# Two compares of a sine range reduction and three operations of a rounding chain, given from VectorE to GpSimd, in a two-layer transformer block on eight cores

## What is computed

```python
# layer 0, feed-forward (d_model 1024, d_ff 4096)
hidden = x @ W1 + b1
imag = w_imag * sin(theta + hidden * 0.1)
phase = cos(theta) * w_real + sin(theta) * w_imag
y = relu(hidden + phase * imag * 0.1) @ W2 + b2
# layer 1, attention: K and V are fake-quantized
k = fake_quant(k, scale, zero); v = fake_quant(v, scale, zero)
#   fake_quant: q = clip(round(x / scale + zero), 0, 255); (q - zero) * scale
# layer 1, feed-forward: 16 experts, top 2, plus a shared expert
```

## Time and profile before

| | us |
|---|---|
| median of 2 timed runs | 7583.97 (7529.44 to 7638.49) |
| the profiled execution, its own time | 7332.9 |
| its span, slowest core | 7331.3 |
| its span, fastest core | 7310.8 |
| PE busy, DVE busy, ACT busy, POOL busy | 4706.4, 2767.5, 2083.8, 170.7 |

### The profile page before, as it was taken

The page is one execution under the profiler, slowest core; times in us unless marked ns, Lnnn a source line. Parts: engine busy times, 40 slices in busy tenths (PEclk is TensorE's granted clock), DMA queues, the critical chain, the costliest instruction groups (busy, mean ns, idle before and its releaser), DMA issues.

```text
span 7331.3 us, 65020 instructions; the slowest of 8 cores (7310.8 to 7331.3 us)
## 1 busy us (share of the span) xinstructions
PE 4706.4 (64%) x17489; PEld 1733.7 (24%) x17489; DVE 2767.5 (38%) x4355; ACT 2083.8 (28%) x3175; POOL 170.7 (2%) x186
## 2 busy tenths in 40 slices
PE   1555777873255855735434667773599999998772
PEld 0211222221011311301111122221244444443230
DVE  2524422215544344346434333235433334332114
ACT  2233344533343144222122455633111111111012
POOL 0000000000000000000000000000000000000000
PEclk8777888986565866865556788886799999999885
DMA  1111000000011511400001110000222222222321
GB/s 50 24 18 12 5 8 9 1 12 0 12 19 22 55 20 18 41 12 12 0 0 15 12 12 9 1 12 0 35 35 35 35 35 35 35 35 37 55 46 46
DMA packets 236271, 160.88 MB, mean 22 GB/s; under 512 B 138921, under 2 KB 225494, under 8 KB 233878
## 3 DMA queue, kind: packets, MB, share of 16 engines
q0 software_dynamic: 232320, 138.92, 14.0%
q1 hardware_dynamic: 3606, 17.79, 0.7%
HBM read 287.21 MB, written 8.39 MB: 40 GB/s over the span
## 4 chain that ended last, share of the span: by engine, by line
PE 52%; DVE 25%; ACT 11%; issue 6%; DMA 5%; DVEq 1%; SPq 0%; ACTq 0%; POOL 0%; POOLq 0%
PE ps L305 36%; PE ps L301 15%; DVE SMALLF L323 6%; ACT SQR L332 3%; DVE B1f L323 2%; DVE FQR L323 2%; DVE B4f L323 2%; DMA WBq<-w_qkv 1%; DVE SCpa L323 1%; DVE B2f L323 1%; ACT HID L332 1%; ACT B1f L332 1%; DVE X L323 1%; DMA WBm<-ws_u 1%; ACT SINB L332 1%
## 5 line engine op out<-in xcount | busy, mean ns | idle before, releaser
L305 PE MATMUL ps<-XB,WBm 128*128 128x512 bf16 x4480 | 1117.9, 391 | 64.1 <-DMA WBm<-ws_g 52.8
L305 PE MATMUL ps<-PT,ARV 128*64 128x512 bf16 (+2 forms) x1152 | 485.5, 421 | 391.5 <-DVE XB L323 268.6
L305 PE MATMUL ps<-XB,WBf 128*128 128x512 bf16 x896 | 374.3, 588 | 430.4 <-ACT B0f L332 373.6
L332 ACT ACTIVATE SGR<-ps 128x512 bf16<-128x512 f32 x320 | 191.1, 597 | 1580.8 <-PE ps L301 888.9
L305 PEld LDWEIGHTS ps<-XB,WBm 128*128 128x128 bf16 x4480 | 446.1, 100 | 632.7 <-issue 135.5
L305 PE MATMUL ps<-HPAIR,WBm 128*128 128x512 bf16 x2272 | 546.7, 384 | 59.7 <-DMA WBm<-ws_d 59.7
L332 ACT ACTIVATE PT<-ps,BIASC 128x512 bf16<-128x512 f32 (+3 forms) x640 | 398.9, 623 | 492.8 <-PE ps L301 358.8
L323 DVE TENSOR_TENSOR ps<-ps,CTRI 128x128 f32<-128x128 f32 x512 | 153.5, 300 | 1015.6 <-PE ps L301 987.3
L332 ACT ACTIVATE PT<-ps,BIA 128x512 bf16<-128x512 f32 (+3 forms) x640 | 399.0, 623 | 394.7 <-PE ps L301 227.5
L301 PE MATMUL ps<-PT,CONES 128*128 128x512 bf16 (+3 forms) x1280 | 495.5, 387 | 0.0
L323 DVE RECIPROCAL SMALLF<-ps 64x512 f32<-64x512 f32 x128 | 429.4, 3355 | 65.4 <-PE ps L301 49.6
(11 more groups left out here) (225 smaller groups left out, 5166.7 us busy)
## 6 DMA issues: line engine op xcount, KB each, us to landing
WBf<-w_ff POOLq DMA_DIRECT2D x32, 1024.0 KB, 9.8
WBq<-w_qkv POOLq DMA_DIRECT2D x64, 256.0 KB, 4.7
WBm<-we_g POOLq DMA_DIRECT2D x16, 1024.0 KB, 9.4
WBm<-we_u POOLq DMA_DIRECT2D x16, 1024.0 KB, 13.5
WBm<-we_d POOLq DMA_DIRECT2D x16, 1024.0 KB, 10.7
X<-x SPq DMA_DIRECT2D x1, 8192.0 KB, 34.2
WBkv<-w_qkv POOLq DMA_DIRECT2D x8, 1024.0 KB, 9.3
WBm<-ws_g POOLq DMA_DIRECT2D x8, 1024.0 KB, 8.3
```

The costliest lines, as they stand in the source:

```text
L305: E.matmul(o, l, r, start=a, stop=b, tile_position=t))
L332: getattr(E, nm)(*a, **k).then_inc(sA.h, 1))
```

## The change

A new helper `gop` does for GpSimd what `vop` does for VectorE. In `fakequant` the two casts and the difference go from VectorE to GpSimd, and VectorE's next operation waits for them. In `ffn0` the two compares (`B4` = ...) go to GpSimd, each between operations that stay on VectorE. Added waits keep the buffers safe.

```diff
+        def gop(name, *args, waits=(), **kw):
+            P.em("gpsimd", lambda E, v=sG.n: E.wait_ge(sG.h, v))
+            for (sem, val) in waits:
+                P.wait("gpsimd", sem, val)
+            v = sG.inc()
+            P.em("gpsimd", lambda E, nm=name, a=args, k=kw:
+                 getattr(E, nm)(*a, **k).then_inc(sG.h, 1))
+            return v
...
-                        vop("tensor_copy", FQI[:, :], FQY[:, :], waits=((sA, a1),))
-                        vop("tensor_copy", FQR[:, :], FQI[:, :])
-                        vop("tensor_tensor", FQY[:, :], FQY[:, :], FQR[:, :],
-                            ALU.subtract)
+                        g1 = gop("tensor_copy", FQI[:, :], FQY[:, :],
+                                 waits=((sA, a1), (sV, use.get("fq", 0)),
+                                        (sA, use.get("fq_aev", 0))))
+                        gop("tensor_copy", FQR[:, :], FQI[:, :])
+                        g3 = gop("tensor_tensor", FQY[:, :], FQY[:, :], FQR[:, :],
+                                 ALU.subtract)
                         vop("tensor_scalar", FQC[:, :], FQY[:, :], 0.5, None,
-                            ALU.is_ge)
+                            ALU.is_ge, waits=((sG, g3),))
...
-                                vop("tensor_scalar", B4[:, qsl], B1[:, qsl],
-                                    math.pi, None, ALU.is_ge, waits=((sA, a_t),))
-                                vop("scalar_tensor_tensor", B1[:, qsl], B4[:, qsl],
-                                    -TWO_PI, B1[:, qsl], ALU.mult, ALU.add)
-                                vop("tensor_scalar", B4[:, qsl], B1[:, qsl],
-                                    -math.pi, None, ALU.is_lt)
+                                g1 = gop("tensor_scalar", B4[:, qsl],
+                                         B1[:, qsl], math.pi, None, ALU.is_ge,
+                                         waits=((sA, a_t),))
+                                v1 = vop("scalar_tensor_tensor", B1[:, qsl],
+                                         B4[:, qsl], -TWO_PI, B1[:, qsl],
+                                         ALU.mult, ALU.add, waits=((sG, g1),))
+                                g2 = gop("tensor_scalar", B4[:, qsl], B1[:, qsl],
+                                         -math.pi, None, ALU.is_lt,
+                                         waits=((sV, v1),))
                                 vv = vop("scalar_tensor_tensor", B1[:, qsl],
                                          B4[:, qsl], TWO_PI, B1[:, qsl], ALU.mult,
-                                         ALU.add)
+                                         ALU.add, waits=((sG, g2),))
```

More of the change, by code:

```diff
@@ L694, in fakequant @@
                         use["fq"] = vq
-                        return aop("activation", dst_ap, FQR[:, :], AF.Identity,
-                                   scale=KVC[:, 2:3], bias=KVC[:, 3:4],
-                                   waits=((sV, vq),))
+                        a_ev2 = aop("activation", dst_ap, FQR[:, :], AF.Identity,
+                                    scale=KVC[:, 2:3], bias=KVC[:, 3:4],
+                                    waits=((sV, vq),))
+                        use["fq_aev"] = a_ev2
+                        return a_ev2
                     wq = dram[wqname].rearrange("(c p) n -> p c n", p=128)
```

## The result

The changed kernel is slower: the ratio of its time to that of the kernel before is 1.071, with a 95% interval of 1.060 to 1.082. The median over all timed runs is 8119.3 us (7887.8 to 8310.7, 11 runs); for the kernel before, over 10 runs, 7492.0 us. The forecast was 8072. The spans are 7331.3 us (before) and 7886.7 us (after). The difference to explain is 555 us; the sum on record was 488.

A forecast was written before the change was run, and what follows sets the result against it. Bound: a chain of non-overlapping steps hopping between engines, none full. Compares +197, fakequant +73 and late loads +218 make +488 us on the timed median 7584: 8072 us, range 7700 to 8350.

The forecast's parts named there:

- the sum on record: Whole kernel: compares +197, fakequant +73 and late loads +218 make +488 us.
- The base of 7584: Median of the timed runs before, 251 us above the profiled 7333; the change touches nothing in that distance.
- The chain: ffn0 and fakequant: steps hop between engines without overlap, so added time counts in full, 128 and 64 times.
- Part 1: ffn0's 256 compares on POOL: 0.55 us start, 0.75 work, 0.10 out, 0.77 more each, +197 us.
- My wrong-if bound: ffn0: a POOL compare under 0.45 or over 1.3 us breaks part 1.
- Part 2: fakequant's three moved operations: 3.10 us instead of 1.96 in each of 64 steps, +73 us.
- Part 3: Weight loads queued behind POOL's new work leave late: ffn0 slabs 151, W2 42, K and V 25, +218 us.
- the 26.6 us: Start of W2: third matmul group starts 26.6 us after the last compare instead of 5.4, costing 21.2, twice.
- POOL is as quick as DVE: Rival for the moved operations: they cost nothing extra, late loads remain, +218, 7802 us; 0.16 together with loads not late.
- POOL is dear: Rival for the moved operations: about twice VectorE's ordinary rate, 1.36 us each, +761, 8345 us; chance 0.16.
- The relief counts: Rival: POOL's compare runs beside DVE's other step, DVE loses 248 us of work, 7336 us; chance 0.04.
- The signs I named: ffn0: first-half window 426 to about 600 us, sine wait 4.3, PE idle on WBf about 16 times, some 10 us each.

The follow-up runs named there:

- ffn_only: Against the changed kernel, fakequant's three operations back on VectorE, only ffn0's compares on GpSimd; span 7794.0 us, +463 on the kernel before.
- fq_only: Against the changed kernel, ffn0's compares back on VectorE, only fakequant's three operations on GpSimd; span 7427.6 us, +96 on the kernel before.
- late_loads: Kernel before, all vector work on VectorE, each slab load also waiting for the previous slab's last compare or difference; span 7530.2 us, +199.
- early_loads: Changed kernel with slab loads emitted one slab earlier, ahead of the running slab's GpSimd work; span 7703.7 us, 183 less than the changed kernel.
- pipe_pool: early_loads with ScalarE's and VectorE's lists in ffn0 reordered so steps overlap, compares and fakequant operations still on GpSimd; span 7186.3 us on core 4.
- pipe_casts: Kernel before with overlapping steps in ffn0 and fakequant, only fakequant's two casts on GpSimd, WBkv loads one slab early; ratio 0.917, span 6755.7 us.
- micro: All four stages left out; single operations timed on GpSimd and VectorE, alone and together; GpSimd compare 1.49 us, cast 0.61, VectorE compare 0.43.

## Why the prediction was right, point by point

**The number.** 8072 against 8119 is closer than the reasoning deserves. The sum was 488 us and the spans show 555. The base of 7584 was the median of two runs; over ten it is 7492, and 7492 + 488 would have been 7980. I had said that nothing in the change touches the distance of the timed runs from the profiled one. It was 159 us before (7492 against 7333) and 231 after (8119 against 7888), for which no run here shows a reason. These misses happened to make up for each other.

**The chain.** Right. Every nanosecond between `B0` and the sine went to the end 128 times, in `fakequant` 64 times. `ffn_only` and `fq_only` show the parts to be additive.

**Part 1, the compares: the mechanism right, the term mis-sized by 89 us, from two errors of opposite sign.** I took 0.55 us to get in and 0.75 of work. Measured: 0.15 and 1.49, so 0.40 too much and 0.74 too little, 256 times. The 0.55 came from a load's issue; it is real for a load (0.54 in `late_loads`) and wrong for an ordinary operation. The 0.75 came from the middle of ordinary rows on other engines, and one of them misled: the 0.90 us of `X<-X,COLS` is a mean of two kinds. Timelines of DVE and POOL of the kernel before:

```profile
2451.97 1.65 DVE L323 TENSOR_SCALAR X<-X,COLS 128x512 f32<-128x512 f32 x1 [0.18 <-DVE X L323]
...
2458.88 0.49 DVE L323 TENSOR_SCALAR X<-X,COLS 128x512 f32<-128x512 f32 x1 [0.18 <-DVE X L323]
```

```profile
2451.71 1.68 POOL L277 DMA_DIRECT2D WBf<-w_ff  x1 [12.29 <-PE ps L301]
```

It takes 0.49 us alone and 1.65 while GpSimd issues a load, which itself takes 1.68 us where others take 0.87. The row was no price of an operation but one of a collision, and it stood in the trace before. My wrong-if bound (a compare over 1.3 us breaks part 1) was crossed: part 1 as priced is broken, its place in the chain is not.

**Part 2, fakequant.** +70 for +73, by luck in its inside: 0.19 to get in instead of 0.55, casts 0.61, difference 1.26, together 3.06 us from `FQY`'s end to VectorE's next operation for my 3.10.

**Part 3, the late loads.** Right in all three places, 196 for 218. `late_loads` shows 199 us of it without any GpSimd work, `early_loads` gives 183 back. The surplus was the 0.55 us delay, which a load behind GpSimd's own work does not pay, and a landing of 8.9 to 9.4 us in the slabs where I used the median 9.8. At W2 the 26.6 us came out to the digit, but by luck: the load landed 11.2 us after its start, not 9.8, and the cold group took 8.36, not 9.35.

**The rivals.** "POOL is as quick as DVE" fell. "POOL is dear" held for the work of a compare, 1.49 us where it said 1.36, and not for the casts (0.61); with the short start a compare cost 1.75 us in the chain, between my 1.40 and its 2.01. On the Trainium skill (GPSIMD Engine Reference, § 3.1 Elementwise): its ratio of 1.96 is for a two-input operation, and for that one this trace agrees, 1.26 us against 0.69, a ratio of 1.8; for an operation with a constant the ratio here is 1.49 to 0.43, or 3.5, and for a cast 1.4. "The relief counts" fell in the order of the program, and for the compares in the order of `pipe_pool` too; it holds for the casts in `pipe_casts`.

**The signs I named.** The window over the first half grew to about 635 us, where I wrote 600; ACT's sine waits 4.98 for my 4.3; PE waited for `WBf` 17 times, 16 of them with the load right behind a compare. But I had said "some 10 us each" of those waits, and they are 45: I had put the chain's loss, not PE's idle time.

## What to carry to other kernels

Before moving an operation to an idle engine, ask whether it lies in a chain of steps that do not overlap. If it does, the idle engine's lower load is worth nothing and its price and handovers count in full, and it is the order of the lists that has to change: here the order alone gave 7%. And look at what else that engine's list holds, because a load emitted behind new work leaves late even if the queue is idle.

## What the runs showed of the hardware that I had not expected

- On GpSimd, an operation with one constant on 128x512 takes 1.49 us, a copy or cast 0.61, a float32 difference of two inputs 1.26; the types made no difference in the pairs that `micro` compares. An ordinary operation starts 0.15 to 0.19 us after its release, a load 0.53 to 0.54.
- VectorE and GpSimd slow each other when they run at once: a compare on VectorE from 0.43 to 0.65 or 0.67, a two-input operation from 0.69 to 0.96, and on GpSimd a compare from 1.49 to between 1.66 and 1.99. While GpSimd issued a load, a VectorE compare took 1.51 us and an operation `X<-X,COLS` 1.65 (0.49 alone), and the issue 1.67 instead of 0.87; six other meetings of the same kind cost a compare only 0.1 us.
- With steps that overlap, the granted clock in `ffn0` rose from 0.62 to 0.97 although PE does the same matmuls: in the kernel before, PE stood idle between the steps' groups of eight, and ran them near the lower level.
